# Four graph layers on 32 graphs: the third norm and its transposes earlier in the written-out order

## The chip, the cores and the metric

The kernel runs on one core of a Trainium2 chip. The metric is device time in microseconds of one execution of the whole program. Every kernel computes the same 32 graphs from HBM to HBM.

## The reference

Thirty-two graphs of N = 256 nodes with F = 256 features, an adjacency matrix of 256 x 256 per graph and a node mask. Four layers follow one another, each added to its input and normalised over the features:

```
x1 = layernorm(x  + relu([x, adj@x / deg] @ W0^T))
x2 = layernorm(x1 + gcn3(x1, adj, W1, b1, W2, b2, W3, b3))
x3 = layernorm(x2 + attention(x2, mask, adj, W_qkv, W_out, b_out))     # 8 heads of 64
x4 = layernorm(x3 + softmax_over_nodes(gate(x3, adj, W_qk)) * (x3 @ W_v^T))
```

In the attention the probabilities are 0.33 (softmax(q k^T / 8) + adj + exp(-adj)). The gate of a node is the sum over its row of adjacency times q k^T / 8. The output is x4.

## The kernel before

**Precision and tiles.** A graph is held as two tiles of 128 partitions. Matmuls that need float32 precision are made of three passes of a faster type: each operand is split into a high part (a ScalarE copy, functions ending in `_hi`) and a low part (a VectorE subtraction, functions ending in `_lo`), and `product` multiplies high by high, high by low and low by high. Several products are cut in a HI part, which needs only the high half of the late operand, and a LO part. Transposes (`transpose_tiles`, L1517) are four TensorE instructions of 128 x 128 into one PSUM bank, and are followed by the `_hi` and `_lo` reads of that bank.

**Order.** Nothing schedules at run time. Each engine has its own order, written out by hand: `first_graphs`, then `slot(s)` for s = 5 to 32, then `last_graphs`. Calls for graphs outside 0 to 31 do nothing. A slot interleaves the stages of five or six graphs, one graph at each stage. The slots of the engines are offset: for the third norm, TensorE transposes x3 of graph s-4 in its slot s (L1875), ScalarE handles graph s-3 in its slot s (L636, L641), VectorE takes the mean of graph s-5 (L1181), GpSimd makes the reciprocal deviation of graph s-2 (L362). Since the offsets differ, the step from slots to `last_graphs` falls at a different graph on each engine: TensorE's last slot has x3 of graph 28, ScalarE's last slot has x3 of graph 29, GpSimd's last slot has x3 of graph 30, and VectorE's last slot has the mean of graph 27.

**The path of x3.** `attention_out` (L1091, VectorE) adds bank 4 to x2 and the bias and writes `x3_pre`. `norm_stats(2)` and `norm_mean(2)` (VectorE) give mean and variance. `norm_rstd(2)` (L342, GpSimd) adds epsilon, takes the power -0.5, negates the mean and multiplies: four small instructions, the last of which writes `centre`. `norm_apply(2)` (L587, ScalarE) writes x3 in two instructions. `x3_transpose` (L1777, TensorE) transposes it into bank 4, after a wait until VectorE has read the scores of pair 2 out of that bank. `x3_hi` and `x3_lo` split it into `x3T`. `tail_project` HI and LO (L1784) multiply it with the weights of the last layer; `tail_qkv` (ScalarE) copies the result, from which VectorE and TensorE work out the gate. `tail_out` (L1140) reads x3 again.

**Around it.** In TensorE's slot the order at that place is: `qk(3)` of one graph, `gate_column`, the transposes of the probabilities of pairs 0 and 1 (`probs_t`, four calls), with the transposes of x2 of the next graph before the last of them, `scores(2)`, `scores(3)`, `attend(0)`, `attend(1)`, `x3_transpose`, `qk(0)` of the next graph, `tail_project` HI, `mix` HI and LO, `tail_project` LO. VectorE reads the scores of pair 2 (L1061) as soon as TensorE has them, then applies the first norm (`norm_apply(0)`, L932) and then writes the low part of x2T (`x2_lo`), on which `qk(0)` waits. In `last_graphs` TensorE transposes x3 of graph 29 after `attend(30, 1)`, and `qk(31, 2)` waits for `tail_qkv(29)` on ScalarE. Transpose of the probabilities of pair 1, head half 1, waits until ScalarE has copied those of pair 0, head half 0, since both use bank 6.

Of the kernel before, what the change touches and what calls it, by code (L numbers as in the profile page):

```python
# [13 lines left out]
def graph_blocks_kernel(nc, x_d, adj_d, nodemask, xT_d, adjT_d, w0_d, w123_d, L1_b1, L1_b2, L1_b3, wqkv_d, wout_d,  # L14
# [22 lines left out]
    with ctx:  # L37
        def sb(name, shape, dt=F32):
            return ctx.enter_context(nc.sbuf_tensor(name, shape, dt))
# [70 lines left out]
        sb("space_2", [P, HALF // 2])  # L110
        oT = [sb(f"oT_{s}", [P, PAIRS, N], F32R) for s in "hl"]
        x3_pre = sb("x3_pre", [P, NT, F])
        x3 = sb("x3", [P, NT, F])


        x3T = [sb(f"x3T_{s}", [P, FT, N], F32R) for s in "hl"]
# [43 lines left out]
        X2T = 3  # L160
        VALUES = 6
        Y = 4
        X3T = 4
        PROJ3 = 0
        ADJK = 4
        GATE_ROW = 5
# [57 lines left out]
        def once(g):  # L224
            return min(g + 1, G)
# [13 lines left out]
        def reuse(eng, semaphore, n):  # L239

            if n > 0:
                eng.wait_ge(semaphore, n)
# [88 lines left out]
        @block.gpsimd  # L331
        def _(pool):
            nc.gpsimd.memset(one[:, :], 1.0)
            nc.gpsimd.memset(eps[:, :], LN_EPS)
            nc.gpsimd.memset(minus_half[:, :], -0.5).then_inc(pool_const, 1)
            nc.gpsimd.memset(ident[:, :], 0.0).then_inc(pool_ident, 1)
            pool.wait_ge(pool_ident, 1)
            nc.gpsimd.affine_select(out=ident[:, :], in_=ident[:, :], compare_op=ALU.not_equal, fill=1.0,
                                    base=0, pattern=[[-1, P]], channel_multiplier=1).then_inc(pool_ident, 1)
            pool.wait_ge(pool_const, 1)  # L340

            def norm_rstd(k, g):  # L342
                if not live(g):
                    return
                pool.wait_ge(dve_mv[k], once(g))
                nc.gpsimd.tensor_tensor(mv[:, k, :, 1], mv[:, k, :, 1], eps[:, :], ALU.add) \  # L346
                    .then_inc(pool_var[k], 1)
                pool.wait_ge(pool_var[k], once(g))
                nc.gpsimd.tensor_tensor(rstd[:, k], mv[:, k, :, 1], minus_half[:, :], ALU.pow) \  # L349
                    .then_inc(pool_rstd[k], 1)  # L350
                if k >= 2:
                    nc.gpsimd.tensor_scalar(minus_mean[:, k - 2], mv[:, k, :, 0], -1.0, None, ALU.mult) \
                        .then_inc(pool_minus[k - 2], 1)
                    pool.wait_ge(pool_minus[k - 2], once(g))
                    pool.wait_ge(pool_rstd[k], once(g))
                    nc.gpsimd.tensor_tensor(centre[:, k - 2], minus_mean[:, k - 2], rstd[:, k], ALU.mult) \
                        .then_inc(pool_centre[k - 2], 1)

            def slot(s):
                norm_rstd(3, s - 4)  # L360
                norm_rstd(1, s)
                norm_rstd(2, s - 2)  # L362
                norm_rstd(0, s + 1)

            def first_graphs():
                norm_rstd(0, 0)
                norm_rstd(0, 1)
                norm_rstd(1, 0)
                norm_rstd(0, 2)
                norm_rstd(1, 1)  # L370
                norm_rstd(1, 2)
                norm_rstd(2, 0)
                norm_rstd(0, 3)
                norm_rstd(2, 1)
                norm_rstd(1, 3)
                norm_rstd(0, 4)
                norm_rstd(3, 0)
                norm_rstd(1, 4)
                norm_rstd(2, 2)
                norm_rstd(0, 5)  # L380

            def last_graphs():
                norm_rstd(3, G - 3)
                norm_rstd(2, G - 1)
                norm_rstd(3, G - 2)
                norm_rstd(3, G - 1)

            first_graphs()
            for s in range(FIRST, LAST):
                slot(s)  # L390
            last_graphs()

        @block.scalar
        def _(act):
# [167 lines left out]
            def x3_hi(g):  # L562
                if not live(g):
                    return
                act.wait_ge(pe_x3T, once(g))
                copy(x3T[0][:, :, :], halves(bank(X3T))).then_inc(act_x3T, 1)

# [19 lines left out]
            def norm_apply(k, g):  # L587
                if not live(g):
                    return
                act.wait_ge(pool_centre[k - 2], once(g))  # L590
                if k == 2:
                    reuse(act, dve_x4_pre, once(g - 1))
                if k == 3:
                    reuse(act, dma_out[g % 2], 16 * (g // 2))
                src, dst = ((x3_pre, x3), (x4_pre, y_sb[:, g % 2]))[k - 2]
                for t in range(NT):
                    last = nc.scalar.activation(dst[:, t], src[:, t], ACT.Identity,  # L597
                                                bias=centre[:, k - 2, t:t + 1], scale=rstd[:, k, t:t + 1])
                last.then_inc(act_y if k == 3 else act_x3, 1)

            def slot(s):
                probs_t(s - 3, 2, 0)
                probs_t(s - 3, 2, 1)
                hidden(0, s - 1)
                hidden_hi(0, s - 1)
                probs_t(s - 3, 3, 0)
                probs_t(s - 3, 3, 1)
                out_hi(s - 3, 2)
                x_hi(s)
                degrees(s)  # L610
                exps(s - 2, 0, 0)
                out_hi(s - 3, 3)
                gate_exps(s - 4)
                sup_hi(1, s - 1)
                exps(s - 2, 0, 1)
                qk_hi(s - 2, 2)
                exps(s - 2, 1, 0)
                hidden(1, s - 1)
                hidden_hi(1, s - 1)
                adj_exp(s)  # L620
                exps(s - 2, 1, 1)
                mask_bias(s - 1)
                adj_hi(s)
                norm_apply(3, s - 5)
                sup_hi(2, s - 1)
                sup0_hi(s)
                values(s - 2)
                self_copy(s)
                qk_hi(s - 2, 3)
                gate_column(s - 4)  # L630
                probs_t(s - 2, 0, 0)
                probs_t(s - 2, 0, 1)
                probs_t(s - 2, 1, 0)
                probs_t(s - 2, 1, 1)
                x2_hi(s - 1)
                norm_apply(2, s - 3)  # L636
                exps(s - 2, 2, 0)
                exps(s - 2, 2, 1)
                out_hi(s - 2, 0)
                x1_hi(s)  # L640
                x3_hi(s - 3)  # L641
                exps(s - 2, 3, 0)
                qk_hi(s - 1, 0)
                exps(s - 2, 3, 1)
                sup_hi(0, s)
                tail_qkv(s - 3)
                out_hi(s - 2, 1)
                qk_hi(s - 1, 1)

            def first_graphs():  # L650
# [137 lines left out]
                mask_bias(3)  # L788
                sup0_hi(4)
                values(2)  # L790
                qk_hi(2, 3)
                gate_column(0)
                probs_t(2, 0, 0)
                probs_t(2, 0, 1)
                x2_hi(3)
                probs_t(2, 1, 0)
                probs_t(2, 1, 1)
                exps(2, 2, 0)
                exps(2, 2, 1)
                norm_apply(2, 1)  # L800
                x3_hi(1)
                x1_hi(4)
                out_hi(2, 0)
                out_hi(2, 1)
# [61 lines left out]
        def _(dve):  # L866
# [273 lines left out]
            def tail_out(g):  # L1140
                if not live(g):
                    return
                dve.wait_ge(act_gate_col, once(g))
                reuse(dve, act_y, once(g - 1))
                dve.wait_ge(act_x3, once(g))
                for t in range(NT):
                    last = V_.scalar_tensor_tensor(out=x4_pre[:, t], in0=qkv3[:, t, 2 * D:L3C],
                                                   scalar=gate_col[:, t:t + 1], in1=x3[:, t],
                                                   op0=ALU.mult, op1=ALU.add)
                last.then_inc(dve_x4_pre, 1)  # L1150

            def slot(s):
# [23 lines left out]
                sup_lo(2, s - 3)  # L1176
                norm_stats(2, s - 5)
                probs(s - 4, 1, 1)
                gcn_out(s - 3)
                sup0_lo(s - 2)  # L1180
                norm_mean(2, s - 5)  # L1181
                norm_stats(1, s - 3)
                norm_mean(1, s - 3)
                aggregate(s - 2)
# [308 lines left out]
        def _(pe):  # L1493
# [283 lines left out]
            def x3_transpose(g):  # L1777
                if not live(g):
                    return
                pe.wait_ge(dve_scores, nth2(g + 1, 2, 1))  # L1780
                pe.wait_ge(act_x3, once(g))
                transpose_tiles(bank(X3T), x3).then_inc(pe_x3T, 1)

            def tail_project(g, part):  # L1784
                if not live(g):
# [47 lines left out]
            def slot(s):  # L1833
# [33 lines left out]
                probs_t(s - 3, 0, 1)  # L1867
                probs_t(s - 3, 1, 0)
                x2_transpose(s - 2)
                probs_t(s - 3, 1, 1)  # L1870
                scores(s - 3, 2)
                scores(s - 3, 3)
                attend(s - 3, 0)
                attend(s - 3, 1)
                x3_transpose(s - 4)  # L1875
                qk(s - 2, 0)
                tail_project(s - 4, HI)
                mix(s - 1, HI)
# [255 lines left out]
```

## Time and profile before

| | us |
|---|---|
| median of 3 runs | 1295.74 |
| lowest and highest | 1294.81, 1297.44 |
| the profiled execution, its own time | 1296.16 |
| its span, first to last instruction | 1294.4 |
| TensorE busy | 1269.5 (98%) |
| VectorE busy | 1160.8 (90%) |
| ScalarE busy | 969.8 (75%) |
| GpSimd busy | 179.3 (14%) |

The granted TensorE clock is 0.998 of full speed over the span. The steady part repeats a slot of 39.07 us for each graph. Times in timelines are microseconds from the first instruction of the span. Matmul rows show a start and a modelled duration that overlaps the next ones, so on TensorE the distance from start to start is read, not the duration.

### The profile page before, as it was taken

How to read it: one execution, taken by the hardware profiler on the slowest of the kernel's cores; microseconds unless marked ns; L12 is line 12 of the kernel's file. 1: busy time of each engine (PE TensorE's matmuls, PEld its weight loads, DVE VectorE, ACT ScalarE, POOL GpSimd, SP SyncE). 2: the span in 40 equal slices, each digit the busy share in tenths (PEclk: the TensorE clock that was granted, in tenths of full speed). 3: DMA queues.
4: the chain of work that ended last, by engine and by line, in shares of the span. 5: the costliest groups of instructions: out<-in, count | busy, mean ns of one | idle time of the engine just before them, and what ended most of it. 6: DMA issues, size and time to landing. Idle time of an engine off the chain costs nothing.

```text
span 1294.4 us, 30393 instructions
## 1 busy us (share of the span) xinstructions
PE 1269.5 (98%) x10848; PEld 1162.2 (90%) x10848; DVE 1160.8 (90%) x3661; ACT 969.8 (75%) x2573; POOL 179.3 (14%) x393
## 2 busy tenths in 40 slices
PE   7999999999999999999999999999999999999996
PEld 7898899999999999999999999999999999999985
DVE  7988999999999999999999999999999999998984
ACT  7677777778778778778778777787777787777773
POOL 0100111101111101111101111101111111111101
PEclk9999999999999999999999999999999999999999
DMA  6110111110111110111110111100111100110000
GB/s 227 34 35 2 35 43 43 44 43 1 43 43 43 43 43 2 43 43 43 43 31 14 43 43 43 43 26 19 43 44 43 43 17 28 43 43 10 10 9 25
DMA packets 34309, 49.02 MB, mean 38 GB/s; under 512 B 7920, under 2 KB 16880, under 8 KB 34160
## 3 DMA queue, kind: packets, MB, share of 16 engines
q1 hardware_dynamic: 34160, 47.08, 11.5%
q8 instruction: 88, 1.44, 0.5%
q14 instruction: 61, 0.50, 0.1%
HBM read 38.68 MB, written 8.39 MB: 36 GB/s over the span
## 4 chain that ended last, share of the span: by engine, by line
PE 94%; ACT 2%; DVE 2%; DMA 1%; POOL 1%; issue 1%; SPq 0%; ACTq 0%; POOLq 0%; DVEq 0%
PE psum L1506 63%; PE psum L1520 11%; PE psum L1756 9%; PE psum L1714 8%; PE psum L1807 1%; PE psum L1810 1%; PE psum L1819 1%; ACT work L545 1%; DMA adjT_sb<-in_adjT 1%; PE psum L1830 0%; ACT x L597 0%; POOL rstd L349 0%; DVE bn L902 0%; DMA v_sb<-in_w 0%; DVE work L1080 0%
## 5 line engine op out<-in xcount | busy, mean ns | idle before, releaser
L545 ACT ACTIVATE work<-work,shift 128x256 f32<-128x256 f32 x512 | 253.2, 498 | 5.5 <-DVE shift L1061 5.5
L1080 DVE SCALAR_TENSOR_TENSOR work<-work,rsum,extra 128x256 f32<-128x256 f32 x512 | 217.0, 475 | 1.0
L396 ACT ACTIVATE work<-psum 128x512 f32<-128x512 f32 x256 | 138.1, 595 | 73.3 <-PE psum L1520 69.4
L1061 DVE CUSTOM_DVE_ANT_0 work<-psum,minus_big 128x256 f32<-128x256 f32 x512 | 189.5, 417 | 3.3 <-PE psum L1714 3.2
L346 POOL TENSOR_TENSOR mv<-mv,eps 128x2 f32<-128x2 f32 x128 | 31.0, 243 | 1094.4 <-DVE mv L923 1094.4
L396 ACT ACTIVATE sup_h<-psum 128x512 fp32r<-128x512 f32 x124 | 73.3, 591 | 117.8 <-PE psum L1506 117.5
L1506 PE MATMUL psum<-x2T_h,wqkv_h 128*128 128x256 f32 x512 | 145.7, 285 | 0.0
L1506 PE MATMUL psum<-x2T_l,wqkv_h 128*128 128x256 f32 x512 | 143.0, 279 | 0.0
L1506 PE MATMUL psum<-x2T_h,wqkv_l 128*128 128x256 f32 x512 | 142.8, 279 | 0.0
L1520 PE MATMUL psum<-ident,work 128*128 128x128 f32 x1024 | 129.0, 274 | 0.0
L1756 PE MATMUL psum<-work,v_sb 128*64 128x256 f32 x1024 | 124.7, 385 | 1.0 <-ACT work L396 1.0
L396 ACT ACTIVATE qkT_h<-psum 128x512 fp32r<-128x512 f32 x128 | 75.3, 589 | 55.9 <-PE psum L1506 55.7
L1520 PEld LDWEIGHTS psum<-ident,work 128*128 128x128 f32 x1024 | 113.0, 141 | 1.4 <-DVE work L1080 0.6
L349 POOL TENSOR_TENSOR rstd<-mv,minus_half 128x2 f32<-128x2 f32 x128 | 106.9, 835 | 10.0
L1756 PEld LDWEIGHTS psum<-work,v_sb 128*64 128x64 f32 x1024 | 67.9, 136 | 37.4 <-ACT work L396 1.4
L873 DVE TENSOR_TENSOR sup_l<-psum,sup_h 128x512 fp32r<-128x512 f32 x124 | 85.0, 686 | 14.4 <-ACT sup_h L396 14.2
L545 ACT ACTIVATION_READ_ACCUMULATOR work<-work,shift 128x1 f32 x512 | 97.3, 190 | 0.0
L1506 PEld LDWEIGHTS psum<-x2T_h,wqkv_h 128*128 128x128 f32 x512 | 96.5, 188 | 0.5 <-DVE x2T_l L873 0.2
L1506 PEld LDWEIGHTS psum<-x2T_l,wqkv_h 128*128 128x128 f32 x512 | 96.8, 189 | 0.0
L1506 PEld LDWEIGHTS psum<-x2T_h,wqkv_l 128*128 128x128 f32 x512 | 96.3, 188 | 0.0
L902 DVE BATCH_NORM_STATS2 bn<-x_pre 128x6 f32<-128x256 f32 x256 | 94.9, 414 | 0.3
L873 DVE TENSOR_TENSOR qkT_l<-psum,qkT_h 128x512 fp32r<-128x512 f32 x128 | 86.6, 678 | 3.0 <-ACT qkT_h L396 3.0
(185 smaller groups left out, 3794.3 us busy)
## 6 DMA issues: line engine op xcount, KB each, us to landing
xT_sb<-in_xT SPq DMA_DIRECT2D x32, 256.0 KB, 2.6
adjT_sb<-in_adjT SPq DMA_DIRECT2D x32, 256.0 KB, 2.9
adj_sb<-in_adj SPq DMA_DIRECT2D x32, 256.0 KB, 4.5
x_sb<-in_x SPq DMA_DIRECT2D x32, 256.0 KB, 4.7
out<-y_sb SPq DMA_DIRECT2D x32, 256.0 KB, 4.5
work<-in_wqkv SPq DMA_DIRECT2D x1, 1536.0 KB, 10.5
mask_row<-in_nodemask SPq DMA_DIRECT2D x32, 32.0 KB, 4.5
w_raw<-in_w SPq DMA_DIRECT2D x3, 256.0 KB, 5.7
```

Of the source, the lines that this page charges most:

```text
L346: nc.gpsimd.tensor_tensor(mv[:, k, :, 1], mv[:, k, :, 1], eps[:, :], ALU.add) \
L349: nc.gpsimd.tensor_tensor(rstd[:, k], mv[:, k, :, 1], minus_half[:, :], ALU.pow) \
L396: return nc.scalar.activation(dst, src, ACT.Copy, scale=scale)
L545: last = nc.scalar.activation(prob[:, p % 2, i, h], prob[:, p % 2, i, h], ACT.Exp, bias=shift[:, p % 2, h, i:i + 1], scale=-1.0, accum_out ...
L873: return V_.tensor_tensor(dst, src, f32(hi_part), ALU.subtract)
L902: last = V_.bn_stats(out=bn[:, k, t], in_=src[:, t])
L1061: last = V_.tensor_tensor_reduce(out=prob[:, p % 2, i, h], in0=bank(SCORES[p] + h)[:, i * N:(i + 1) * N], in1=minus_big[:, g % 2, i], scal ...
L1080: last = V_.scalar_tensor_tensor(out=prob[:, p % 2, i, h], in0=prob[:, p % 2, i, h], scalar=rsum[:, p % 2, h, i:i + 1], in1=extra[:, g % 2 ...
L1506: last = mm(dst, left, right, start=opens and n == 0, stop=closes and n == len(steps) - 1)
L1520: last = nc.tensor.transpose(dst[:, r * N + t * P:r * N + (t + 1) * P], src[:, t, block_of(r)], ident[:, :])
L1714: last = mm(bank(SCORES[p] + h)[:, i * N:(i + 1) * N], qkT[left][rows, p % 2, 0, block_of(i)], qkT[right][rows, p % 2, 1], start=n == 0 an ...
L1756: last = mm(bank(PV[p])[h * D:(h + 1) * D, 0:N], v_sb[:, k, (2 * p + h) * D:(2 * p + h + 1) * D], probT[:, p % 2, h, k], start=k == 0, sto ...
```

## The change

- The third norm's `x3` has two buffers; ScalarE waits with writing graph g for VectorE's `tail_out` of graph g-2 instead of g-1.
- Its transposes go to PSUM bank 2 instead of bank 4. The wait for the scores of pair 2 goes, and a wait for ScalarE's copy of the self part of graph g+3 (`act_self`, also bank 2) takes its place.
- TensorE's slot: `x3_transpose` moves from behind `attend(1)` to between the transposes of x2 and the last `probs_t`. TensorE's `first_graphs` and `last_graphs` are not edited.
- ScalarE's slot: `norm_apply(2)` moves from behind `x2_hi` to behind `self_copy`; `x3_hi` moves from behind `x1_hi` to behind `x2_hi`. In `first_graphs` the same for graph 1.
- VectorE's slot: `norm_mean(2)` moves ahead of `gcn_out`.
- GpSimd's slot: `norm_rstd(2)` moves ahead of `norm_rstd(1)`.

```diff
@@ tiles and banks @@
-        x3 = sb("x3", [P, NT, F])
+        x3 = sb("x3", [P, 2, NT, F])
...
-        X3T = 4
+        X3T = 2
@@ gpsimd, norm_rstd @@
             def slot(s):
                 norm_rstd(3, s - 4)
+                norm_rstd(2, s - 2)
                 norm_rstd(1, s)
-                norm_rstd(2, s - 2)
                 norm_rstd(0, s + 1)
@@ scalar, norm_apply @@
                 if k == 2:
-                    reuse(act, dve_x4_pre, once(g - 1))
+                    reuse(act, dve_x4_pre, once(g - 2))
@@ scalar, slot @@
                 self_copy(s)
+                norm_apply(2, s - 3)
                 qk_hi(s - 2, 3)
                 gate_column(s - 4)
                 probs_t(s - 2, 0, 0)
...
                 x2_hi(s - 1)
-                norm_apply(2, s - 3)
+                x3_hi(s - 3)
                 exps(s - 2, 2, 0)
                 exps(s - 2, 2, 1)
                 out_hi(s - 2, 0)
                 x1_hi(s)
-                x3_hi(s - 3)
@@ scalar, first_graphs @@
                 values(2)
+                norm_apply(2, 1)
                 qk_hi(2, 3)
...
                 x2_hi(3)
+                x3_hi(1)
                 probs_t(2, 1, 0)
                 probs_t(2, 1, 1)
                 exps(2, 2, 0)
                 exps(2, 2, 1)
-                norm_apply(2, 1)
-                x3_hi(1)
@@ vector, slot @@
                 probs(s - 4, 1, 1)
+                norm_mean(2, s - 5)
                 gcn_out(s - 3)
                 sup0_lo(s - 2)
-                norm_mean(2, s - 5)
@@ tensor @@
             def x3_transpose(g):
-                pe.wait_ge(dve_scores, nth2(g + 1, 2, 1))
+                pe.wait_ge(act_self, once(g + 3))
                 pe.wait_ge(act_x3, once(g))
-                transpose_tiles(bank(X3T), x3).then_inc(pe_x3T, 1)
+                transpose_tiles(bank(X3T), x3[:, g % 2]).then_inc(pe_x3T, 1)
@@ tensor, slot @@
                 x2_transpose(s - 2)
+                x3_transpose(s - 4)
                 probs_t(s - 3, 1, 1)
                 scores(s - 3, 2)
                 scores(s - 3, 3)
                 attend(s - 3, 0)
                 attend(s - 3, 1)
-                x3_transpose(s - 4)
                 qk(s - 2, 0)
```

## Rows read from the trace of the kernel before

**Rows 1.** Busy by stretch: length, then PE, PEld, DVE, ACT, POOL, granted clock.
```profile
182.10:1158.90 976.80, 976.80 (x8403) 898.05 (x8403) 899.03 (x2853) 749.28 (x2003) 142.18 (x300) 1.00 0.12 36
```
**Rows 2.** Timeline of TensorE, one slot: start, us, line, out<-in, count.
```profile
606.86 0.60 PE L1520 MATMUL psum<-ident,x 128*128 128x128 f32 x4
607.29 0.60 PE L1520 MATMUL psum<-ident,work 128*128 128x128 f32 x4
...
608.38 0.39 PE L1714 MATMUL psum<-qkT_h,qkT_l 64*128 64x256 f32 x4
...
611.29 0.66 PE L1520 MATMUL psum<-ident,x 128*128 128x128 f32 x4
611.70 0.36 PE L1506 MATMUL psum<-x2T_h,wqkv_h 128*128 128x256 f32 x1
611.90 0.28 PE L1506 MATMUL psum<-x2T_l,wqkv_h 128*128 128x256 f32 x1
...
613.05 0.28 PE L1506 MATMUL psum<-x2T_h,wqkv_l 128*128 128x256 f32 x1
613.27 0.44 PE L1506 MATMUL psum<-w_h,x3T_h 128*128 128x384 f32 x1
613.55 0.34 PE L1506 MATMUL psum<-w_l,x3T_h 128*128 128x384 f32 x1
```
**Rows 3.** Timeline of ScalarE, the same slot; idle time in brackets.
```profile
605.39 0.60 ACT L396 ACTIVATE qkT_h<-psum 128x512 fp32r<-128x512 f32 x1 [1.30 <-PE psum L1506]
...
608.90 1.09 ACT L597 ACTIVATE x<-x_pre,centre,rstd 128x256 f32<-128x256 f32 x2
...
612.63 0.58 ACT L396 ACTIVATE x3T_h<-psum 128x512 fp32r<-128x512 f32 x1
```
**Rows 4.** Timeline of VectorE, the same slot.
```profile
601.65 0.69 DVE L1040 TENSOR_TENSOR x_pre<-psum,x_b 128x512 f32<-128x512 f32 x1 [0.47 <-PE psum L1506]
...
608.82 0.42 DVE L1061 CUSTOM_DVE_ANT_0 work<-psum,minus_big 128x256 f32<-128x256 f32 x1
...
610.85 0.68 DVE L873 TENSOR_TENSOR x2T_l<-psum,x2T_h 128x512 fp32r<-128x512 f32 x1
```
**Rows 5.** Timeline of GpSimd, the third norm in the same slot.
```profile
605.07 0.19 POOL L346 TENSOR_TENSOR mv<-mv,eps 128x2 f32<-128x2 f32 x1
...
606.70 0.19 POOL L356 TENSOR_TENSOR centre<-minus_mean,rstd 128x2 f32<-128x2 f32 x1
```
**Rows 6.** Timeline of TensorE and VectorE, x3 of graph 1.
```profile
143.33 0.28 PE L1506 MATMUL psum<-x2T_l,wqkv_h 128*128 128x256 f32 x1
...
140.76 0.69 DVE L873 TENSOR_TENSOR x2T_l<-psum,x2T_h 128x512 fp32r<-128x512 f32 x1
```
**Rows 7.** Timeline of GpSimd near 134 us, of VectorE near 1190 us.
```profile
133.14 0.19 POOL L346 TENSOR_TENSOR mv<-mv,eps 128x2 f32<-128x2 f32 x1 [34.20 <-DVE mv L923]
...
134.37 0.19 POOL L356 TENSOR_TENSOR centre<-minus_mean,rstd 128x2 f32<-128x2 f32 x1
...
1189.67 0.38 DVE L923 BATCH_NORM_AGGREGATE mv<-bn 128x2 f32<-128x6 f32 x4
...
1191.01 0.74 DVE L932 TENSOR_SCALAR x<-x_pre,mv,rstd 128x256 f32<-128x256 f32 x2
```
**Rows 8.** Timeline of VectorE, ScalarE and TensorE in the last order.
```profile
1224.67 0.24 DVE L923 BATCH_NORM_AGGREGATE mv<-bn 128x2 f32<-128x6 f32 x2
...
1226.38 0.60 ACT L396 ACTIVATE qkT_h<-psum 128x512 fp32r<-128x512 f32 x1 [1.89 <-PE psum L1506]
...
1232.26 0.49 ACT L545 ACTIVATE work<-work,shift 128x256 f32<-128x256 f32 x1
...
1237.51 0.81 ACT L396 ACTIVATE qkv<-psum 128x768 f32<-128x768 f32 x1
...
1232.55 0.66 PE L1520 MATMUL psum<-ident,x 128*128 128x128 f32 x4
...
1238.72 0.28 PE L1506 MATMUL psum<-x2T_h,wqkv_h 128*128 128x256 f32 x1
```

More of the change, by code:

```diff
@@ L591, in norm_apply @@
                 if k == 2:
-                    reuse(act, dve_x4_pre, once(g - 1))
+                    reuse(act, dve_x4_pre, once(g - 2))
                 if k == 3:
                     reuse(act, dma_out[g % 2], 16 * (g // 2))
-                src, dst = ((x3_pre, x3), (x4_pre, y_sb[:, g % 2]))[k - 2]
+                src, dst = ((x3_pre, x3[:, g % 2]), (x4_pre, y_sb[:, g % 2]))[k - 2]
                 for t in range(NT):
@@ L1147, in tail_out @@
                     last = V_.scalar_tensor_tensor(out=x4_pre[:, t], in0=qkv3[:, t, 2 * D:L3C],
-                                                   scalar=gate_col[:, t:t + 1], in1=x3[:, t],
+                                                   scalar=gate_col[:, t:t + 1], in1=x3[:, g % 2, t],
                                                    op0=ALU.mult, op1=ALU.add)
```

## The prediction

> **What bounds the kernel now.** I read the busy time by stretch first, then the timeline of TensorE in one slot, then those of the other engines at the same place. Between 182 and 1159 us TensorE is busy 976.80 of 976.80 us, at full granted clock, while VectorE has 899.03 and ScalarE 749.28 [rows 1]. These are 25 slots of 39.07 us. A slot is TensorE's stream of instructions, and the change, which adds and removes no matmul, can act on the steady part only through short waits that the modelled ends hide. They are found by start-to-start distances. In the slot at 611 us [rows 2] the last layer's first matmul starts at 613.27, 0.22 us behind its predecessor at 613.05, where the ten steps before that, from 611.90, took 0.12 each; it is also 0.44 long where the next is 0.34. ScalarE's `x3_hi` ends at 612.63 + 0.58 = 613.21 [rows 3], 0.05 before the first: this is a wait of 0.10 + 0.10 = 0.20 us per slot. TensorE's other irregular distances there belong to changes of operand type and tile size, and stay.
>
> The second thing to see is what is nearly late. VectorE starts on the scores of pair 2 at 608.82, and TensorE finishes them at 608.38 + 0.39 = 608.77 [rows 2, 4]: 0.05 later, so VectorE is there just in time, and is released by TensorE. From there it runs without a pause to `x2_lo`, which ends at 610.85 + 0.68 = 611.53. `qk(0)` needs that, and starts at 611.70 [rows 2]. The slack is 0.17 us less the 0.05 of a hand-over, some 0.12 us, and the four x3 transposes at 611.29 stand in between: they cover this chain.
>
> **Steady slots, graphs 2 to 27 (26 of them).** The four transposes cost TensorE 607.29 - 606.86 = 0.43 us wherever they stand [rows 2]; their sum is unchanged. But in the new place they precede the scores, so scores of pair 2 end at 609.20, VectorE starts them at 609.25, and `x2_lo` ends at 611.53 + 0.43 = 611.96. TensorE has by then done `attend(0)` and `attend(1)` 0.43 later but has no transposes left, and would be ready at about the old 611.70. It must wait: `qk(0)` starts at 611.96 + 0.05 = 612.01. A first matmul after a wait is followed 0.10 later than usual, as at 613.27, so the second one starts at 612.01 + 0.12 + 0.10 = 612.23 instead of 611.90: 0.33 us late. The old wait of 0.20 goes, since `x3_hi` now runs before the exponentials, about 609.4. Sum: 0.33 - 0.20 = +0.13 us per slot, 26 x 0.13 = **+3.4 us**. The bounds come from the hand-over and refill (0.04 each way): 0.08 to 0.18 per slot, 2.1 to 4.7 us.
>
> The other moved pieces cost nothing in a slot. `norm_mean(2)` falls into VectorE's idle 0.47 us before `gcn_out` [rows 4]. GpSimd then starts the norm at about 601.4, and its four instructions took 606.70 + 0.19 - 605.07 = 1.82 us [rows 5]: `centre` is ready at 603.2. `norm_apply(2)`, 1.09 us, fits in ScalarE's idle 1.30 before 605.39 [rows 3]; the next cover would be gone if `centre` came after about 604.3, and then `qk_hi(3)`, the copies and the scores of pair 3 would all be late. The exponentials of pair 2 gain 1.09 and lose the 0.43 of the later last copy and the 0.58 of `x3_hi`, and wait for VectorE's later scores: some 0.2 us late by this working, on no path to TensorE. VectorE's 0.43 is used up again before `tail_k`, where it waits for ScalarE's copy of the last layer, which follows TensorE. The second x3 buffer and the wait on `act_self` (a copy that ScalarE makes ahead of the norm itself) cost nothing; neither does bank 2. No DMA and no queue of SP is touched.
>
> **Graph 1**, the first transposed in a slot. TensorE waited there for ScalarE's norm, which stood behind two pairs of exponentials; both move in front, so that wait goes. Then VectorE decides here too: `x2_lo` ends at 140.76 + 0.69 + 0.43 = 141.88, the second matmul of `qk(0)` starts at 141.88 + 0.05 + 0.22 = 142.15 instead of 143.33 [rows 6]: **-1.2 us** (-1.0 to -1.4). Graph 0 stands in unedited orders and keeps its wait.
>
> **Graph 28**: the orders of the engines disagree. VectorE already is in `last_graphs`, where `norm_mean(1, 30)` precedes `norm_mean(2, 28)` in one row of four instructions [rows 7], but GpSimd's slot now takes the third norm first. So `rstd` for x2 of graph 30 comes after the whole third norm: mean at 1189.67 + 0.38 = 1190.05, hand-over 0.08, third norm 134.37 + 0.19 - 133.14 = 1.42 [rows 7] to 1.82 [rows 5], then about 1.0 for the two instructions of the other norm (1.42 less two short ones of 0.2, as the last there): 1192.6 to 1193.0. VectorE's `norm_apply(1)` stood at 1191.01, so it and all behind it wait 1.6 to 2.0 us. The old wait of 0.20 at the last layer goes, and I take as much for idle time of VectorE that is used up on the way, an estimate. With the short norm: **+1.2 us** (0.9 to 1.7).
>
> **Graph 29**: ScalarE's slot has the new order, TensorE's `last_graphs` the old one. First, `norm_apply(2, 29)` now stands before `qk_hi(30, 3)`, and its mean ends at 1224.67 + 0.24 [rows 8]. With 0.08 and 1.42 to 1.82 `centre` is at 1226.4 to 1226.8, the norm takes 1.09 and `qk_hi` moves from 1226.38 to 1227.5 to 1227.9. The copies of the probabilities behind it shift by that, and so do TensorE's last `probs_t` (same bank as the first), hence the x3 transposes, from 1232.55 to 1233.6 to 1234.0. Second, `x3_hi(29)` now stands before the exponentials of pair 2, so ScalarE waits for those transposes: `x3_hi` starts at about 1234.2, exponentials at 1234.7 instead of 1232.26, and `tail_qkv` follows 5.25 - 0.58 = 4.7 behind them, at 1239.4, and ends 0.81 later at 1240.2 [rows 8]. `qk(31, 2)` waits for it: 1240.2 to 1240.6 instead of 1238.72. With the slow norm, since VectorE is at work beside it as in the steady slot [rows 5]: **+1.8 us** (0.6 to 2.4, the low end if the ScalarE delay is half absorbed).
>
> What lengthens GpSimd's norm shows in 1.82 against 1.42 us for the same four instructions [rows 5, 7]. The Trainium skill (SBUF — State Buffer, Who interferes with whom) says that GpSimd and VectorE share a port pair under an exclusive lock, taken by VectorE instructions with two SBUF inputs or in a two-port mode. In the new steady place VectorE reads one operand from PSUM, so by that rule the norm would be short there, at graph 28 also, and long at graph 29, where `probs` reads two SBUF operands: the same total as mine; with the lock never in the way the total would be 0.4 us less.
>
> **Sum.** +3.4 - 1.2 + 1.2 + 1.8 = +5.2 us on the profiled execution's own 1296.16 us (span 1294.4 and 1.8 around it), or 1301.4. That execution is 0.4 above the median of the runs, so against the median 1295.74 I say 1300.9. This case alone spans +2.2 to +7.8 us: 1297.9 to 1303.5. A measurement of this kernel can tell about 0.2%, 2.6 us, from no change.
>
> **Rivals.** (1) Faster. The chain from scores to `x2_lo` does not hold `qk(0)`, for instance because VectorE finds the scores early enough. Then each steady slot keeps the full gain of 0.20: 26 x -0.20 = -5.2, with -1.2 and +3.0 at the ends -3.4 us, 1292.3. It decides where `x2_lo` ends before about 611.65. For it: the removed wait is certain. Against it: 608.82 follows 608.77, and nothing between it and `x2_lo` can be skipped. Chance 0.12. (2) Balance. The new wait costs what the old one did (0.20: TensorE is itself slower from `attend` to `qk` without transposes between, or the refill is hidden): steady part 0, ends +1.8, 1297.5. Chance 0.13. (3) Much slower. `centre` comes later than 604.3 in every slot and `qk_hi(3)` becomes late; at 0.4 us per slot this adds 10, 1311. The 1.1 us between 603.2 and 604.3 speak against it. Chance 0.06. (4) My forecast, 0.69.
>
> The range 1296.5 to 1303.5 holds (4) and (2), 0.82. Faster by over 0.2% is (1), 0.12; within it is (2) and a little, 0.14; slower is the rest, 0.74.
>
> **What would show it.** Right: a slot of 39.20 us; `qk(0)` starting 0.05 behind the end of `x2_lo`; VectorE idle about 0.4 us before the scores of pair 2; no wait at the last layer's first matmul; the wait for graph 1's norm gone; near 1191 VectorE idle for the rstd of x2, near 1240 TensorE idle for `tail_qkv`. Wrong: a slot of 39.07 or less, or ends whose waits are not there.

## The result and the profile after

The changed kernel takes 1304.09 us (median of 4, 1303.08 to 1305.54) against 1295.90 for the kernel before on the same chip: a ratio of 1.0062 [1.0047, 1.0077], 8.2 us slower. The prediction was 1300.9, in a range of 1296.5 to 1303.5. The sign and most of the mechanism came true; the time lies 0.6 above the range. The profiled execution took 1304.37 us, with a span of 1302.6, 8.2 over the span of before. TensorE is busy 1270.6 us where it was busy 1269.5: almost all of the 8.2 us is time without a matmul, or hidden under a modelled end.

The chain of the page and the steady stretch, which answers to [rows 1]:

```profile
PE 85%; DVE 8%; ACT 3%; issue 2%; POOL 1%; DMA 1%; SPq 0%; ACTq 0%; POOLq 0%; DVEq 0%
```
```profile
185.10:1165.00 979.90, 974.15 (x8398) 897.04 (x8398) 899.92 (x2849) 751.38 (x2000) 133.56 (x300) 1.00 0.12 36
```

VectorE had 2% of the chain before; it has 8% now. TensorE was busy for the whole of the steady stretch before and now lacks 5.75 us in 25 slots, 0.23 per slot. Which wait that is, the list of waits tells (us in total, times, longest):

```profile
PEld psum L1506 <- DVE x2T_l L873: 19.2, 29, 0.8
...
DVE work L1061 <- PE psum L1714: 13.6, 29, 1.2
...
ACT x L597 <- POOL centre L356: 9.5, 4, 3.2
...
PE psum L1506 <- DVE x2T_l L873: 6.3, 27, 0.3
...
DVE x L932 <- POOL rstd L349: 2.9, 3, 1.5
```

TensorE waits for `x2_lo` 27 times, for 6.3 us; before, that group wasn't there at all. VectorE waits for the scores of pair 2 29 times where it was 5 times (3.2 us). ScalarE waits for a `centre` four times, once before. One slot of TensorE, to be laid beside [rows 2]:

```profile
610.18 1.04 PE L1520 MATMUL psum<-ident,x 128*128 128x128 f32 x8
611.05 0.60 PE L1520 MATMUL psum<-ident,work 128*128 128x128 f32 x4
...
612.86 0.40 PE L1714 MATMUL psum<-qkT_h,qkT_l 64*128 64x256 f32 x4
613.19 1.95 PE L1756 MATMUL psum<-work,v_sb 128*64 128x256 f32 x16
...
615.37 0.39 PE L1506 MATMUL psum<-x2T_h,wqkv_h 128*128 128x256 f32 x1 [0.23 <-DVE x2T_l L873]
...
616.77 0.28 PE L1506 MATMUL psum<-x2T_h,wqkv_l 128*128 128x256 f32 x1
616.89 0.37 PE L1506 MATMUL psum<-w_h,x3T_h 128*128 128x384 f32 x1
617.09 0.34 PE L1506 MATMUL psum<-w_l,x3T_h 128*128 128x384 f32 x1
```

And VectorE in the same slot, which answers to [rows 4]:

```profile
612.60 0.42 DVE L1061 CUSTOM_DVE_ANT_0 work<-psum,minus_big 128x256 f32<-128x256 f32 x1 [0.44 <-PE psum L1714]
...
614.63 0.68 DVE L873 TENSOR_TENSOR x2T_l<-psum,x2T_h 128x512 fp32r<-128x512 f32 x1
```

The x8 at 610.18 are the transposes of x2 and x3 in a row. VectorE is idle for 0.44 us before the scores, ends `x2_lo` at 614.63 + 0.68 = 615.31, and `qk(0)` starts at 615.37, with an idle time of its own. The last layer's first matmul follows its predecessor by 616.89 - 616.77 = 0.12: the wait of before is gone.

**Where the 8.2 us are.** I took TensorE's start of the second matmul of the last layer (L1790) for each graph, in both traces, and the difference of the two:

| graph | step of the difference, us | predicted |
|---|---|---|
| 0 | +1.28 | 0 |
| 1 | -1.16 | -1.2 |
| 2 | +1.77 | +0.13 |
| 3 to 27 | +3.67 (0.147 each) | +3.25 (0.13 each) |
| 28 | +1.01 | +1.2 |
| 29 and 30 | +1.60 | +1.8 |
| 31 | +0.02 | 0 |
| sum | +8.19 | +5.2 |

Two lines are off by more than 0.5 us: graph 0, which is no work of the change (see further down), and graph 2. Graph 2 is in the code. ScalarE and GpSimd there:

```profile
177.31 1.09 ACT L597 ACTIVATE x<-x_pre,centre,rstd 128x256 f32<-128x256 f32 x2 [2.83 <-POOL centre L356]
178.31 0.57 ACT L396 ACTIVATE qkT_h<-psum 128x512 fp32r<-128x512 f32 x1
```
```profile
174.38 0.20 POOL L346 TENSOR_TENSOR mv<-mv,eps 128x2 f32<-128x2 f32 x1 [20.96 <-DVE mv L923]
174.65 0.70 POOL L349 TENSOR_TENSOR rstd<-mv,minus_half 128x2 f32<-128x2 f32 x1
175.32 0.19 POOL L346 TENSOR_TENSOR mv<-mv,eps 128x2 f32<-128x2 f32 x1
175.59 1.34 POOL L349 TENSOR_TENSOR rstd<-mv,minus_half 128x2 f32<-128x2 f32 x1
176.77 0.21 POOL L352 TENSOR_SCALAR minus_mean<-mv 128x2 f32<-128x2 f32 x1
177.08 0.19 POOL L356 TENSOR_TENSOR centre<-minus_mean,rstd 128x2 f32<-128x2 f32 x1
```

GpSimd waits 20.96 us with `norm_rstd(1, 4)`, whose mean comes late, and only then does the third norm of graph 2. In its `first_graphs`, which the change doesn't edit, these two calls stand in the old order, while ScalarE, already in slot 5, has `norm_apply(2, 2)` ahead of `qk_hi(3, 3)`. So `qk_hi` starts at 178.31, after 2.83 us of idling and a norm of 1.09.

The two late places that were predicted are there. Graph 28 on VectorE, and graph 29 on ScalarE and TensorE:

```profile
1198.11 0.74 DVE L932 TENSOR_SCALAR x<-x_pre,mv,rstd 128x256 f32<-128x256 f32 x2 [1.47 <-POOL rstd L349]
```
```profile
1233.19 1.09 ACT L597 ACTIVATE x<-x_pre,centre,rstd 128x256 f32<-128x256 f32 x2 [1.98 <-POOL centre L356]
...
1240.78 0.60 ACT L396 ACTIVATE x3T_h<-psum 128x512 fp32r<-128x512 f32 x1 [1.87 <-PE psum L1520]
...
1245.95 0.80 ACT L396 ACTIVATE qkv<-psum 128x768 f32<-128x768 f32 x1
```
```profile
1246.80 0.39 PE L1506 MATMUL psum<-x2T_h,wqkv_h 128*128 128x256 f32 x1 [0.98 <-ACT qkv L396]
```

### The profile page after: what moved, and what is told of

It is laid out like the page before. It is cut to its first block, busy times and chain, and to the rows that moved or that the text cites. A ratio compares the mean times of both kernels' runs of the same rounds, so it can differ in the third digit from the quotient of the medians.

```text
span 1302.6 us, 30392 instructions
## 1 busy us (share of the span) xinstructions
PE 1270.6 (98%) x10848; PEld 1163.8 (89%) x10848; DVE 1162.3 (89%) x3661; ACT 972.2 (75%) x2573; POOL 170.4 (13%) x393
## 3 DMA queue, kind: packets, MB, share of 16 engines
q1 hardware_dynamic: 34160, 47.08, 11.5%
q8 instruction: 88, 1.44, 0.5%
## 4 chain that ended last, share of the span: by engine, by line
PE 85%; DVE 8%; ACT 3%; issue 2%; POOL 1%; DMA 1%; SPq 0%; ACTq 0%; POOLq 0%; DVEq 0%
PE psum L1506 60%; PE psum L1520 10%; PE psum L1714 6%; PE psum L1756 5%; DVE work L1061 2%; DVE x L932 1%; DVE x2T_l L873 1%; PE psum L1807 1%; ACT work L545 1%; PE psum L1810 1%; PE psum L1819 1%; POOL rstd L349 1%; DVE shift L1061 1%; DVE work L1080 0%; DVE bn L902 0%
## 5 line engine op out<-in xcount | busy, mean ns | idle before, releaser
L349 POOL TENSOR_TENSOR rstd<-mv,minus_half 128x2 f32<-128x2 f32 x128 | 93.9, 734 | 10.0
```

## The experiments

The theory to be tested: (A) a slot loses 0.36 because x3's transposes no longer stand between `attend` and `qk(0)`, where they covered VectorE's chain from scores to `x2_lo`, and gains 0.20 because the norm is early; (B) each place where one engine's unedited order meets another's new slot costs about 1 to 2 us once. The rivals: the 0.15 per slot is the price of eight transposes in a row, of bank 2, or of the new buffer; and the ends are one disturbance that travels.

This table of mean distances from start to start on TensorE, over the slots whose x3 is that of graphs 3 to 27, in ns, is what the slot experiments are read from. "Transposes" is from the first transpose of the probabilities to the scores; then to `attend(0)`; to `qk(0)`'s first matmul; to its second; to the last layer's first; to its second; and on to the next slot.

| kernel | transposes | scores | attend | qk, 1st | qk to last layer | last layer, 1st | rest | slot |
|---|---|---|---|---|---|---|---|---|
| before | 2332 | 1587 | 2296 | 203 | 1368 | 278 | 31005 | 39067 |
| after | 2768 | 1610 | 2177 | 224 | 1286 | 207 | 30941 | 39213 |
| e2_norm_only | 2332 | 1587 | 2296 | 203 | 1273 | 172 | 30993 | 38856 |
| e3_repeat | 2768 | 1610 | 2309 | 224 | 1297 | 175 | 31002 | 39385 |
| e4_behind_scores | 2332 | 2173 | 1877 | 226 | 1295 | 177 | 31021 | 39100 |
| e7_x2_lo_first | 2768 | 1610 | 1877 | 221 | 1543 | 251 | 30948 | 39218 |
| e8_norm_only_mended | 2332 | 1587 | 2297 | 202 | 1272 | 174 | 30967 | 38831 |
| e9_norm0_last | 2768 | 1610 | 1878 | 221 | 1266 | 171 | 31135 | 39049 |
| e10_repeat_norm_only | 2332 | 1587 | 2721 | 201 | 1298 | 178 | 30963 | 39278 |
| e12_buffers_and_bank | 2332 | 1587 | 2296 | 203 | 1374 | 276 | 31007 | 39075 |

What is read from it are the columns up to the last layer. They repeat to a few ns where the order is the same. "Rest" does not: e1, e5 and e6 have the slot orders of the changed kernel and its columns, but 30971, 30987 and 30964 in "rest" instead of 30941, and so slots of 39241, 39257 and 39235. One rival can be read off at once: the eight transposes in a row cost 2768 - 2332 = 436 ns more than four, 109 each, the 0.43 us of [rows 2].

The kernel before gave 1297.58 us beside e1 to e4 and e12, 1295.90 beside e5 to e8 and 1295.96 beside e9 to e11; each ratio is against its own. Diffs are against the changed kernel unless said otherwise.

**The order at graph 2.**

```diff
@@ gpsimd, first_graphs @@
-                norm_rstd(1, 4)
                 norm_rstd(2, 2)
+                norm_rstd(1, 4)
```

> The change with one swap in GpSimd's first_graphs: the third norm of graph 2 ahead of the second norm of graph 4, as its slot has it. Theory (the orders of the engines disagree where first_graphs hands over to the slots): ScalarE no longer sits 2.8 us before the norm of graph 2, the 1.8 us that TensorE lost there go, slots stay at 39.20 us, about 1302.3 us. Rival (graph 2 lost its time to a transfer or to the start of the run): nothing moves, 1304.1 us.

1304.12 us against 1297.58, ratio 1.0050 [1.0035, 1.0065]. The step at graph 2 falls from 1.77 to 0.19 us, and none of those at graphs 1, 28, 29, 30 and 31 moves by more than 0.1. Graphs 3 to 27 together have +4.35 instead of +3.67, all of it in "rest". `centre` is now ready before ScalarE asks for it:

```profile
172.08 0.20 POOL L356 TENSOR_TENSOR centre<-minus_mean,rstd 128x2 f32<-128x2 f32 x1
```
```profile
173.40 1.09 ACT L597 ACTIVATE x<-x_pre,centre,rstd 128x256 f32<-128x256 f32 x2
174.80 0.60 ACT L396 ACTIVATE qkT_h<-psum 128x512 fp32r<-128x512 f32 x1 [0.31 <-PE psum L1506]
```

The 1.58 us are a hand-over between two orders; the intervals of the two ratios overlap, so it is the trace that shows it, not the times.

**The norm alone.** Its calls stay early; transposes and `x3_hi` go back.

```diff
@@ tensor, slot @@
                 x2_transpose(s - 2)
-                x3_transpose(s - 4)
...
                 attend(s - 3, 1)
+                x3_transpose(s - 4)
@@ scalar, slot; in first_graphs likewise for graph 1 @@
                 x2_hi(s - 1)
-                x3_hi(s - 3)
...
                 x1_hi(s)
+                x3_hi(s - 3)
```

> The change with TensorE's transposes of x3 and ScalarE's x3_hi back in their old places; the norm stays early on all engines, bank 2 and the two buffers stay. Theory (the 0.13 us per slot comes from the transposes standing ahead of the scores of pair 2): no wait before qk(0), and x3_hi about 0.3 us earlier than before, so the old wait of 0.20 us goes too: slot 38.87 us; with +1.8 at graph 2, +1.1 at graph 28 and about +1.2 at graph 29, -1.6 at graph 1, about 1293 us. Rival (the early norm itself costs, through ScalarE or the shared norm on GpSimd): slot 39.20 us and about 1302 to 1304 us.

1294.71 us, ratio 0.9978 [0.9969, 0.9988]: faster than before. The table shows both halves of (A) apart. With the transposes back, the first four columns are those of before to the nanosecond; with the norm early, the last layer's first two columns lose 95 and 106 ns, the 0.20 that the prediction read off [rows 2]. So bank 2 and the buffers are not what costs, and the loss belongs to the transposes' place.

**The first two calls of `attend(1)` repeated where cover is missing.** If TensorE really waits before `qk(0)`, work put ahead of it is swallowed.

```diff
@@ tensor, attend @@
+                if p == 1 and 1 <= g <= 29:
+                    for h in range(2):
+                        mm(bank(PV[p])[h * D:(h + 1) * D, 0:N], v_sb[:, 0, (2 * p + h) * D:(2 * p + h + 1) * D],
+                           probT[:, p % 2, h, 0], start=True, stop=True)
```

> The change, with the first two matmuls of attend(1) issued twice for graphs 1 to 29 (same values written again). Adds 0.22 us of TensorE's work per slot right where TensorE is thought to wait 0.30 us for x2_lo. Theory (VectorE's chain from the scores to x2_lo sets the start of qk(0)): slot stays at 39.20 us, about 1304 us. Rival (TensorE's own stream, refill or change of operand type sets it): slot 39.42 us, 29 x 0.22 = 6.3 us more, about 1310 us.

1308.82 us, ratio 1.0086 [1.0071, 1.0101]. The slot grows by 0.172 us, nearer to the rival's 0.22 than to the theory's 0. But the addition was costed too low: each of the two calls leaves two matmuls in the trace, so four were added, and they take 616.05 - 615.61 = 0.44 us:

```profile
615.61 0.60 PE L1756 MATMUL psum<-work,v_sb 128*64 128x256 f32 x4
616.05 1.03 PE L1760 MATMUL psum<-work,v_sb 128*64 128x256 f32 x8
```

So the same addition was also run where nothing waits, on e2:

> e2 (norm early, transposes in the old place, no wait on VectorE there) with e3's repeated matmuls. A control for e3, where they took 0.43 us in the trace and lengthened the slot by 0.17. Theory (in the changed kernel 0.30 us of TensorE's time before qk(0) is a wait for VectorE; in e2 it is not): slot 38.86 + 0.43 = 39.29 us. Rival (repeats overlap with the next matmuls anyway): slot about 39.0 us.

There the same four matmuls cost 425 ns in the column of `attend` and 0.42 us per slot (1305.49 us, one run). In e3 that column grows by only 132: 0.29 us of the 0.425 were swallowed, and the distance from `attend`'s last matmul to `qk(0)` fell from 0.608 to 0.309. This is the wait's size, measured from outside: 0.30 us.

**Transposes behind the scores.** The scores are then as early as before.

```diff
@@ tensor, slot @@
-                x3_transpose(s - 4)
                 probs_t(s - 3, 1, 1)
                 scores(s - 3, 2)
                 scores(s - 3, 3)
+                x3_transpose(s - 4)
                 attend(s - 3, 0)
```

> The change, with the transposes of x3 in TensorE's slot behind scores(3) and ahead of attend(0). Theory: the scores of pair 2 are not delayed and the transposes cover VectorE's chain again; x3_hi still is early enough, so both waits go, against some 0.1 us for one more change between transposes and attend: slot 38.9 to 39.0 us; graph 1 about -1.5, graphs 2, 28 and 29 as in the changed kernel: about 1295 to 1297 us. Rival (any transposes ahead of attend delay qk(0), or ScalarE's wait for them costs): slot 39.1 to 39.3 us, 1301 us or more.

1306.13 us, ratio 1.0065 [1.0050, 1.0080], and a slot of 39.10: I had expected less. The wait before `qk(0)` is gone (1877 where after has 2177) and so is that at the last layer. The slot is as long as the rival said, but for another reason: the four transposes cost 2173 - 1587 = 0.586 us there instead of the 0.436 that they cost among other transposes (2768 - 2332). The time is then also lost at the ends: graph 1 has a step of +0.53 instead of -1.16, graph 28 has +1.59.

**VectorE's order in the slot.** First `x2_lo` ahead of the first norm, then the first norm behind the scores of pair 3.

```diff
@@ vector, slot: e7 @@
-                norm_apply(0, s - 2)
                 x2_lo(s - 1)
+                norm_apply(0, s - 2)
```

> The change with one swap in VectorE's slot: x2_lo ahead of norm_apply(0), which took 0.65 us in front of it. Theory (the chain scores of pair 2, norm_apply(0), x2_lo sets qk(0)): qk(0) starts 0.31 us behind the last matmul of attend(1) instead of 0.61, and the slot falls from 39.21 to 38.87 us, below the 39.07 of before; with the three hand-overs at graphs 2, 28, 29 unmended about 1 to 2 us below the kernel before. Rival (TensorE needs the 0.61 us between attend and qk for itself, or ScalarE sets x2_lo): the slot stays at 39.2 us.

1305.19 us, ratio 1.0068 [1.0055, 1.0082]: no gain, though the wait before `qk(0)` is wholly gone (1877, 0.30 less). It came back as 257 + 44 ns one product later:

```profile
617.48 0.28 PE L1506 MATMUL psum<-x2T_h,wqkv_l 128*128 128x256 f32 x1
617.87 0.41 PE L1506 MATMUL psum<-w_h,x3T_h 128*128 128x384 f32 x1
618.12 0.34 PE L1506 MATMUL psum<-w_l,x3T_h 128*128 128x384 f32 x1
```
```profile
617.29 0.42 DVE L1061 CUSTOM_DVE_ANT_0 work<-psum,minus_big 128x256 f32<-128x256 f32 x1
617.64 0.08 DVE L1061 DVE_READ_ACCUMULATOR2_ANT shift<- 128x1 f32 x1
```

617.87 is 0.39 behind 617.48 where 0.12 is usual. `tail_project` HI writes banks from which VectorE reads the scores of pair 3 (the wait on `dve_scores`, L1791), and VectorE's last read ends at 617.72. That read is as late as before the edit, since the edit only changes the order of what stands ahead of it.

> The change with VectorE's norm_apply(0) behind the scores of pair 3 instead of ahead of x2_lo (e7 had it between the two). e7 took the wait of 0.30 us before qk(0) away and the slot stayed at 39.22, since the last layer's first matmul then stood 0.26 us later: it waits until VectorE has read the scores of pair 3. Theory (VectorE's sequence scores of pair 2, norm_apply(0), x2_lo, scores of pair 3 carries two hand-overs to TensorE, one 0.2 us behind the other): with 0.65 us of it behind both, both waits go, slot about 38.93 us, some 7 us below the changed kernel. Rival (ScalarE, whose x1_hi now comes 1.2 us later and holds up the exponentials of pair 3, or mix, becomes the next gate): slot 39.1 us or more.

1300.09 us, ratio 1.0031 [1.0019, 1.0043], and a slot of 39.05, between the two forecasts. In e9 both gates are open (1878, 1266, 171), which would be worth 0.36 us; the slot gains 0.164, as the rest of it grows by 0.194. ScalarE's `x1_hi`, and behind it VectorE's `fT_l`, now depend on the late norm:

```profile
614.57 0.63 ACT L396 ACTIVATE fT_h<-x 128x512 fp32r<-128x512 f32 x1 [0.97 <-DVE x L932]
```
```profile
616.61 0.28 PE L1506 MATMUL psum<-adjT_l,fT_h 128*128 128x256 f32 x1
616.84 0.74 PE L1506 MATMUL psum<-adjT_h,fT_l 128*128 128x256 f32 x4
```
```profile
PEld psum L1506 <- DVE fT_l L873: 4.6, 27, 0.4
```

A third gate: TensorE's `adjT_h,fT_l` starts 0.23 behind its predecessor, and weight loads wait for `fT_l` in 27 slots, 0.17 each (before: twice). VectorE's sequence carries three hand-overs in a row, and in each of the three orders tried (the changed kernel's, e7, e9) the 0.43 us by which the scores come late are noticed at one of them.

**The last hand-overs.** Both kernels start from e1.

```diff
@@ vector, last_graphs: e5 @@
+                norm_mean(2, G - 4)
                 gcn_out(G - 2)
...
-                norm_mean(2, G - 4)
```

> The change with GpSimd's swap in first_graphs as in e1, and in VectorE's last_graphs norm_mean(2) of graph 28 ahead of gcn_out of graph 30. Theory (graph 28 loses 1.0 us because GpSimd makes the third norm first while VectorE delivers it last): the step from graph 27 to 28 in the trace falls from 0.98 to about 0.2 us, all else as in e1, about 5.5 us over the kernel before. Rival (graph 28 is late because TensorE's last slot itself is longer): the step stays at 1.0 us, about 6.5 us over.

1303.81 us, ratio 1.0059 [1.0045, 1.0073]. The step of graph 28 falls from 0.98 to 0.20. Graph 0 stands 2.18 us late in this execution (next section), and the times can't tell 0.8 us, so this too rests on the trace.

```diff
@@ scalar, slot: e6 @@
                 self_copy(s)
-                norm_apply(2, s - 3)
+                if s < G:
+                    norm_apply(2, s - 3)
...
                 x2_hi(s - 1)
-                x3_hi(s - 3)
+                if s < G:
+                    x3_hi(s - 3)
+                else:
+                    norm_apply(2, s - 3)
...
                 x1_hi(s)
+                if s == G:
+                    x3_hi(s - 3)
```

> The change with e1's swap, and in ScalarE's slot for graph 29 alone the norm and x3_hi in their old places. Theory (ScalarE waits at graph 29 for transposes that TensorE's last_graphs makes late, and qk(31, 2) waits for tail_qkv): the 1.4 us of wait before qk(31, 2) and what precedes it go, to 0.0 to 0.3 us; about 5 us over the kernel before. Rival (those 1.4 us come from VectorE or from the end's own stalls): they stay, about 6.5 us over.

1302.67 us, ratio 1.0047 [1.0033, 1.0061]. The steps of graphs 29, 30 and 31 are 0.06, 0.02 and 0.02 instead of 0.10, 1.43 and 0.00. With e1 and e5 that is (B): three separate places worth 1.6, 0.8 and 1.4 us, each mended with the others unmoved. The changed kernel with all three mended at once was not run.

**No order changed at all**, and only buffers, bank and waits as in the change (diff against the kernel before):

```diff
-        x3 = sb("x3", [P, NT, F])
+        x3 = sb("x3", [P, 2, NT, F])
...
-        X3T = 4
+        X3T = 2
...
-                    reuse(act, dve_x4_pre, once(g - 1))
+                    reuse(act, dve_x4_pre, once(g - 2))
...
-                pe.wait_ge(dve_scores, nth2(g + 1, 2, 1))
+                pe.wait_ge(act_self, once(g + 3))
```

> The kernel before with only the two x3 buffers, bank 2 and the new waits, no order changed. Theory (buffers, bank and waits cost nothing): slot 39.07 us, no step at graphs 1, 2, 28, 29; ratio 1.000 within 0.1%. Any offset at graph 0 is then what one execution's start differs from another's (first matmuls at half the rate for 0.2 to 2 us), not the change. Rival (a part of the loss is the bank's or the buffer's): slot over 39.07 us or a ratio over 1.001.

1298.30 us (n = 11) against 1297.58, ratio 1.0006 [0.9997, 1.0015], a slot of 39.075. Buffers and bank cost nothing that can be told. Its trace nevertheless stands 1.79 us behind that of before at graph 0; graph 0 is taken up in the next section.

**What is worth keeping.** e8 is e2 with the hand-overs of e1, e5 and e6 (only the norm, since `x3_hi` already is in its old place); e11 also moves ScalarE's `x2_hi(2)` and `norm_apply(2, 0)` of `first_graphs` ahead of `exps(1, 2, 0)`.

> e2 (norm early, transposes and x3_hi in their old places) with all three hand-overs mended: e1's swap on GpSimd, e5's move on VectorE, ScalarE's norm of graph 29 in its old place. Theory: slot 38.86 us as in e2 and no steps at graphs 2, 28 and 29: about 6 us below the kernel before, 3.5 below e2. Rival (the steps are part of the early norm, not of the hand-overs): about 3 us below the kernel before, as e2.

> e8 with ScalarE's x2_hi(2) and norm_apply(2, 0) in first_graphs ahead of exps(1, 2, 0). TensorE waits there some 1.2 us for the norm of graph 0 in all kernels so far. Theory: that wait goes and nothing else changes: 1.0 to 1.2 us less than e8, 7 to 8 us below the kernel before. Rival (x2_lo or the exponentials take its place): as e8.

e8: 1289.36 us (1288.56 to 1290.39), ratio 0.9950 [0.9937, 0.9964]. e11: 1288.43 us (1286.23 to 1289.07), ratio 0.9938 [0.9925, 0.9950]. e11 is the best version, 7.5 us under the kernel before; that it beats e8 the intervals don't show, but the wait that it was made for falls from 4.3 us in 3 to 3.3 in 2:

```profile
PE psum L1523 <- ACT x L597: 4.3, 3, 1.8
```
```profile
PE psum L1523 <- ACT x L597: 3.3, 2, 1.8
```

e8 adds up by the trace: -0.236 for each of 25 slots = -5.9, -1.59 at graph 1, -0.23 at graph 2, -0.25 at graphs 28 to 30, and +0.35 from the start give -7.6, the difference of the spans (1286.8 against 1294.4).

## Why the prediction was right and wrong

- **Steady slots**: right. Forecast +0.33 - 0.20 = +0.13; measured +0.36 up to `qk(0)`'s second matmul, -0.15 at the last layer and -0.06 in the rest, +0.147; in e1, e5 and e6, with the same slot orders, it is +0.174, +0.190 and +0.170, as "rest" differs between executions. The old wait was worth the full 0.20 (e2), but 0.05 of it stays in the changed kernel (1286 + 207 against 1273 + 172): there the last layer's first matmul comes just 0.2 behind VectorE's last read of pair 3, the gate that e7 ran into. e3 and e10 size the new wait at 0.30, and e2 shows that undoing the transposes' move removes it. One part of the 0.33 was right by luck: the 0.10 put down to the first matmul after a wait is there without one. `qk(0)`'s second matmul follows its first by 0.221 us in e7 and e9 and by 0.224 and 0.226 in e3 and e4, where nothing waits; it follows by 0.203 behind transposes. So it goes with coming straight from `attend`.
- **Graph 1**: -1.16 for -1.2. **Graph 28**: +1.01 for +1.2. **Graph 29**: +1.60 for +1.8, and the two stages named are in the rows (1233.19, 1240.78, 1246.80). The steps that e1, e5 and e6 take away separately show that these are hand-overs between orders.
- **Graph 2, the step that failed**. The prediction began with "Steady slots, graphs 2 to 27" and let the new norm be ready at 603.2 "in a slot", that is with GpSimd in its slots too. It went through the orders at the end engine by engine and at the start only for graph 1. At graph 2 GpSimd still is in `first_graphs`. It cost 1.77 - 0.13 = 1.6 us. With it the sum is 6.8, and the trace without graph 0's offset has 8.19 - 1.28 = 6.9; what is left of it, +0.4 in the slots and -0.4 at graphs 28 and 29, cancels.
- **Graph 0**: the remaining 1.28 us are the start of this execution and not the change. ScalarE's copy of the attention weights waits for their transfer of 1.5 MB (`in_wqkv`), and TensorE waits behind it. That copy starts at 21.52 in the trace of before and at 22.67 here, 1.15 later. In the twelve other traces it starts 0.12 to 1.53 later than in that of before. In five of them graph 0's offset is 0.1 to 0.3 more than that, as here: 0.23 and 0.33 in e1, 0.77 and 1.03 in e4, 1.25 and 1.40 in e2, and e6 and e8 likewise. In e5, e7 and e12 it is 0.65 to 0.8 more (1.05 and 1.79 in e12, where no order is changed). There the granted clock fell to half speed, 1.2 GHz, for a stretch behind the wait for these weights, as the rows of e5 in the last section show. In e3 and e10 the copy doesn't wait for the transfer, but TensorE is late from a slow start. e9 and e11 have edits that reach graph 0. So the one execution of before that the sum was made against began early. The ratio of the medians gives 8.2 us as well, with an interval of 6.1 to 10.0, so it doesn't contradict the 6.9 that the traces give to the change; which is nearer the runs leave open. The "rest" of e1, e5 and e6 would by itself make it 0.6 to 1.1 more than the 6.9.
- **Rivals**. Faster: it named the gain of 0.20 and the condition that the chain from scores to `x2_lo` doesn't hold `qk(0)`. In the changed kernel it does, by 0.30. e2 meets the condition by another way, and gets the gain. Balance: no, by 0.147 per slot. Much slower: no wait for `centre` in the steady slots, where `qk_hi` still idles 0.32 behind the norm (0.26 to 0.32 in four slots between 568 and 686 us).
- **The share of the port.** In its new place GpSimd's third norm takes 605.98 + 0.19 - 604.73 = 1.44 us where it took 1.82 [rows 5]. VectorE's instruction beside it now has one operand in PSUM; the one beside it before had both in SBUF:

```profile
604.73 0.19 POOL L346 TENSOR_TENSOR mv<-mv,eps 128x2 f32<-128x2 f32 x1 [18.38 <-DVE mv L923]
...
604.97 0.69 DVE L1040 TENSOR_TENSOR x_pre<-psum,x_b 128x512 f32<-128x512 f32 x1 [0.32 <-PE psum L1506]
...
605.98 0.19 POOL L356 TENSOR_TENSOR centre<-minus_mean,rstd 128x2 f32<-128x2 f32 x1
```
```profile
605.17 0.69 DVE L1000 SCALAR_TENSOR_TENSOR x_pre<-x_pre,x_sb 128x512 f32<-128x512 f32 x1
```

  The first fence is the changed kernel's, the second that of before. At graph 2 of the changed kernel the power alone takes 1.34 instead of 0.70, beside the same instruction, there at 175.56. The Trainium skill (SBUF — State Buffer, Who interferes with whom) states that a VectorE instruction with two SBUF inputs contends with a GpSimd instruction that reads SBUF. The traces agree both times. At graph 28 the norm took 1.44 us, short as forecast. At graph 29 the forecast took the long 1.82 and it was 1.55: the power ended before `probs` had run 0.4 us beside it. None of this changed a term of the steady sum, as nobody waits for this norm in a slot.

## What to carry to other kernels

Before work is moved up, ask what it covered where it stood: four transposes of 0.43 us hid a chain on another engine that had 0.12 us of slack, and moving the gate aside by reordering only brought up the next one. Where orders are written out by hand, a reordering has a seam on every engine at both ends of the loop. List, for each moved call, the first and last graph that every engine handles in the new order; each graph at which they disagreed cost 0.8 to 1.6 us once here, and the three of them made about half of the loss. And try the halves of a change alone: the early norm by itself, with seams mended, was worth 6.5 us, and the transposes' move undid it.

## What the runs showed that I had not expected

- The place of four transposes changes their price: 0.436 us among transposes, 0.42 between `attend` and `qk` (2296 in the kernel before less the 1877 of e4), 0.586 between scores and `attend` (e4).
- One call of the source can be more than one matmul on TensorE. The two calls repeated in e3 and e10 are 116 matmuls for 29 graphs, four each, and 4 x 0.108 us, the spacing of the 16 around them, is their 0.43.
- TensorE's first matmuls can run at half rate. In the profiled execution of the changed kernel they follow one another by 0.213 us until 11.5, then by 0.12:

```profile
7.23 0.42 PE L1506 MATMUL psum<-w_l,fT_h 128*128 128x256 f32 x1
7.44 0.41 PE L1506 MATMUL psum<-w_h,fT_h 128*128 128x256 f32 x1
...
11.85 0.28 PE L1506 MATMUL psum<-sup_h,adjT_h 128*128 128x256 f32 x1
11.97 0.28 PE L1506 MATMUL psum<-sup_h,adjT_l 128*128 128x256 f32 x1
```

  This one has 20 such distances there, the kernel before none. The view of the stretch gives a granted clock of 1.00 in both, but the trace's record of the clock only begins at 11.50 us here and at 6.81 in the kernel before, each time where the distances shorten. Ahead of that the 1.00 is no measurement. At 11.85 it is 2.29 us behind the kernel before, but this is used up: at 24.5, behind the wait for the attention weights, 1.15 are left, which is their own lateness.
- In 11 of the 14 traces ScalarE waits for that transfer, and when it is used varies by 1.5 us from one execution to the next:

```profile
22.67 1.49 ACT L396 ACTIVATE wqkv_h<-work 128x1536 fp32r<-128x1536 f32 x1 [0.52 <-DMA work<-in_wqkv]
```
```profile
22.57 1.48 ACT L396 ACTIVATE wqkv_h<-work 128x1536 fp32r<-128x1536 f32 x1 [2.59 <-DMA work<-in_wqkv]
```

  The first is the changed kernel's, the second that of e12.
- The granted clock of TensorE drops to half speed in short stretches of some executions and not of others, whatever the kernel. In e5, after TensorE was idle for 3.08 us behind the late weights, the mean granted clock from 26 to 30 us is 0.57 and the matmuls are 0.21 apart instead of 0.12:

```profile
26.07 0.36 PE L1506 MATMUL psum<-w_h,hidT_h 128*128 128x256 f32 x1 [3.08 <-ACT hidT_h L396]
...
26.57 0.41 PE L1506 MATMUL psum<-w_l,hidT_h 128*128 128x256 f32 x1
26.78 0.41 PE L1506 MATMUL psum<-w_h,hidT_h 128*128 128x256 f32 x1
```

  e7 and e12 have such a stretch at the same place. In e1, e2, e4, e6 and e11 such a stretch lies near the end, between 1270 and 1291 us, and the time behind graph 31's mark is 1.3 to 1.6 us longer than in the kernel before; in the others it is within 0.03. The run times go along: of the 26 runs of e12 and its kernel before, those with a mean clock of 0.999 took 1295.9 to 1297.1 us, those with 0.996 or less 1298.6 to 1300.8. Two traces are therefore compared by steps from graph to graph, not by their ends.
